# Query and key of a fused linear-attention and feed-forward block: seven block products of 256 columns in place of eight

## The reference, cut to what matters

```python
# B, N, C, H = 8, 1024, 256, 16 ; D = C // H = 16 ; INTER = 1024
xn = _layernorm(x, axis=-1)
qkv = (xn @ qkv_w + qkv_b).reshape(b, n, 3, H, D)
q, k = _l2norm(q), _l2norm(k)                  # over the 16 values of a head
kv = jnp.einsum('bhnd,bhne->bhde', k, v)
out = jnp.einsum('bhnd,bhde->bhne', q, kv)
attn = out @ proj_w + proj_b
h = jax.nn.relu(xn @ W1 + b1)
return x + attn + (h @ W2 + b2)
```

## Time and profile before

| | |
|---|---|
| median of 3 runs | 554.02 us (553.8 to 554.61) |
| profiled execution: span on the core | 552.4 us |
| around that span, against the median | 1.6 us |
| TensorE busy | 547.7 us (99%) |
| VectorE busy | 398.5 us (72%) |
| ScalarE busy | 286.9 us (52%) |
| GpSimd busy | 119.4 us (22%) |

### The profile page before, as it was taken

The page is one execution under the profiler, slowest core; times in us unless marked ns, Lnnn a source line. Parts: engine busy times, 40 slices in busy tenths (PEclk is TensorE's granted clock), DMA queues, the critical chain, the costliest instruction groups (busy, mean ns, idle before and its releaser), DMA issues.

```text
span 552.4 us, 8714 instructions
## 1 busy us (share of the span) xinstructions
PE 547.7 (99%) x2590; PEld 460.2 (83%) x2590; DVE 398.5 (72%) x791; ACT 286.9 (52%) x529; POOL 119.4 (22%) x150
## 2 busy tenths in 40 slices
PE   9999999999999999999999999999999999999997
PEld 7888888888888888888888888888888888888896
DVE  6977788567795876858667587775777767684655
ACT  4785654556336563465644556455553655533421
POOL 4242424202052020420213202331024201050100
PEclk9999999999999999999999999999999999999999
DMA  8522134343413434134341343315333251314312
GB/s 259 167 87 50 33 83 93 83 105 83 107 20 86 98 85 95 24 86 98 85 88 31 93 92 84 81 38 113 71 90 67 45 107 38 79 37 93 96 39 76
DMA packets 141413, 45.34 MB, mean 82 GB/s; under 512 B 133330, under 2 KB 136402, under 8 KB 141396
## 3 DMA queue, kind: packets, MB, share of 16 engines
q1 hardware_dynamic: 139280, 44.61, 34.7%
q10 hardware_dynamic: 2116, 0.53, 0.5%
HBM read 20.98 MB, written 8.39 MB: 53 GB/s over the span
## 4 chain that ended last, share of the span: by engine, by line
PE 99%; DVE 0%; issue 0%
PE o_bank L1169 12%; PE o_bank L1170 12%; PE o_bank L1171 12%; PE w_bank L1169 11%; PE w_bank L1170 11%; PE w_bank L1171 11%; PE v_bank L1169 7%; PE v_bank L1170 7%; PE v_bank L1171 7%; PE kv_bank L1307 3%; PE g_bank L1307 3%; PE kv_bank L1312 1%; PE g_bank L1312 1%; PE kv_bank L1323 1%; PE w_bank L1361 1%; PE g_bank L1171 0%
## 5 line engine op out<-in xcount | busy, mean ns | idle before, releaser
L957 DVE SCALAR_TENSOR_TENSOR h_lo<-w_bank,h_hi 128x512 fp32r<-128x512 f32 x128 | 87.4, 683 | 38.2 <-ACT h_hi L607 36.5
L607 ACT ACTIVATE h_hi<-w_bank 128x512 fp32r<-128x512 f32 x128 | 76.4, 597 | 66.5 <-PE w_bank L1171 66.4
L1169 PE MATMUL w_bank<-xT_hi,w_hi 128*128 128x512 f32 x254 | 99.9, 393 | 0.0
L1170 PE MATMUL w_bank<-xT_lo,w_hi 128*128 128x512 f32 x254 | 99.2, 391 | 0.0
L1171 PE MATMUL w_bank<-xT_hi,w_lo 128*128 128x512 f32 x254 | 98.9, 389 | 0.0
L1169 PE MATMUL o_bank<-h_hi,w_hi 128*128 128x512 f32 x240 | 93.5, 389 | 0.0
L1170 PE MATMUL o_bank<-h_lo,w_hi 128*128 128x512 f32 x240 | 93.4, 389 | 0.0
L1171 PE MATMUL o_bank<-h_hi,w_lo 128*128 128x512 f32 x240 | 93.4, 389 | 0.0
L405 POOL TENSOR_TENSOR xn_lo<-xn,xn_hi 128x256 fp32r<-128x256 f32 x56 | 42.5, 759 | 217.6 <-ACT xn_hi L517 213.4
L420 POOL TENSOR_TENSOR y_sb<-y_sb,y_rows 128x256 f32<-128x256 f32 x56 | 52.5, 941 | 123.7 <-DVE y_rows L1001 103.2
L585 ACT ACTIVATE qk_sq<-v_bank 128x512 f32<-128x512 f32 x64 | 38.3, 598 | 72.2 <-PE v_bank L1171 72.2
(11 more groups left out here) (213 smaller groups left out, 921.4 us busy)
## 6 DMA issues: line engine op xcount, KB each, us to landing
y_rows<-blocks SPq DMA_DIRECT2D x256, 32.0 KB, 1.9
x_sb<-x SPq DMA_DIRECT2D x15, 512.0 KB, 3.5
y_sb<-x SPq DMA_DIRECT2D x60, 128.0 KB, 3.3
out<-y_sb SPq DMA_DIRECT2D x58, 128.0 KB, 2.5
xT_raw<-blocks SPq DMA_DIRECT2D x224, 32.0 KB, 1.9
y_sb<-w SPq DMA_DIRECT2D x4, 256.0 KB, 5.1
x_sb<-x SPq DMA_DIRECT2D x2, 256.0 KB, 3.0
w_raw<-w SPq DMA_DIRECT2D x2, 256.0 KB, 7.4
```

Of the source, the lines that this page charges most:

```text
L607: nc.scalar.activation(h_hi[:, j % RING, :], w_bank[j % 2][:], ACT.Relu).then_inc(h_done, 1)
L957: nc.vector.scalar_tensor_tensor(h_lo[:, r, :], w_bank[j % 2][:], 0.0, h_hi[:, r, :].bitcast(F32), ALU.max, ALU.subtract).then_inc(h_lo_do ...
L1169: nc.tensor.matmul(to, left[0], right[0], start=first, stop=False, skip_group_check=shared)
L1170: nc.tensor.matmul(to, left[0], right[1], start=False, stop=False, skip_group_check=shared)
```

## The change

Write the 256 input channels of a tile of tokens as two blocks, and the 512 outputs (q, then k) as two blocks. The product of two tiles with all weights is then a 2 by 2 block product. Before it takes eight block products; after, from half 3 on, seven, with sums and differences of blocks of both factors and of some results (Strassen's product in Winograd's form). Tile n is paired with tile n + 2.

- TensorE: for each pair of tiles, `qk_begin`, `qk_second`, `qk_third` and `qk_fourth` issue 6, 6, 6 and 3 matmuls of 256 columns, where two `query_key` issued 12 of 512. A half has two pairs.
- GpSimd: `x_forms` makes the sums of token blocks (one instruction of 128x512 and two of 128x256, after `move_x` has landed), and `weight_forms`, once, those of the weights. They are kept in `xn` and in `wvp_raw`.
- ACT: `x_forms_high` (128x1024); `qk_seed` (two copies of 128x256, between `qk_begin` and `qk_second`).
- DVE: `x_forms_low` (128x1024); `qk_seed` and `qk_sum` (128x256 each), twice in a half, between the steps of a pair.
- All engines: the `half` of a planned order is replaced by lists written out for the second half, even, odd, last even and last odd halves.
- The call of Bacc has `dynamic_dma_scratch_size=1024`.

```diff
@@ TensorE
+            def qk_begin(s, u, n, batch):
...
+                wait(pe, qk_copied, TILES * s + 2 * n - 1)
+                product(qk_11, (xT_hi[:, u, 0, tile(n)], xT_lo[:, u, 0, tile(n)]),
+                        (wqk_hi[:, 0, 0:C], wqk_lo[:, 0, 0:C]), True, False, shared=True)
+                wait(pe, xf_lo_done, s - FORMS_FROM + 1)
+                qk_form(qk_22, X11_X01, w_form(W_FIVE), n).then_inc(qk_begun, 1)
...
+            def qk_second(s, u, n):
+                wait(pe, qk_seeded, pairs_done(s, n))
+                qk_form(qk_21, X11_X01_X00, w_form(W_SIX), n).then_inc(qk_21_sixth_in, 1)
+                product(qk_11, (xT_hi[:, u, 1, tile(n)], xT_lo[:, u, 1, tile(n)]),
+                        (wqk_hi[:, 1, 0:C], wqk_lo[:, 1, 0:C]), False, True, shared=True)
+
+            def qk_third(s, n):
+                wait(pe, qk_12_seeded, pairs_done(s, n))
+                qk_form(qk_12, X10_X11_X01_X00, (wqk_hi[:, 1, C:2 * C], wqk_lo[:, 1, C:2 * C]), n)
+                qk_form(qk_21, X01_X00, w_form(W_SEVEN), n).then_inc(qk_21_seventh_in, 1)
+
+            def qk_fourth(s, u, n):
+                wait(pe, qk_22_summed, pairs_done(s, n))
...
+            def even_half(b, s):
+                ffn_up(s, 0, 2)
+                ffn_down(s, b, 0, 0)
+                ffn_up(s, 0, 3)
+                ffn_down(s, b, 0, 1)
+                ffn_up(s, 0, 4)
+                ffn_down(s, b, 0, 2)
+                qk_begin(s + 1, 1, 0, b)
+                gather(s, b, 0)
+                qk_second(s + 1, 1, 0)
...
@@ GpSimd
+            def x_forms(s):
+
+                wait(pool, x_moved, 16 * MOVES * (s - 1))
+                first, second = slice(0, PAIR * P), slice(PAIR * P, HALF)
+                nc.gpsimd.tensor_tensor(xf_raw[:, 0:2], xT_raw[:, :, second],
+                                        xT_raw[:, 0].rearrange("p (a n) -> p a n", a=PAIRS),
+                                        ALU.subtract).then_inc(xf_sums_done, 1)
...
@@ DVE
+            def even_half(b, s):
+                divide(0, 0, q_done)
+                xT_low(s + 1, 1)
+                h_low(s, 2)
+                transpose_q(s, 0)
+                x_forms_low(s + 1)
+                k_low(s, 0)
+                h_low(s, 3)
+                variance(s + 2, b + 1, 0)
...
+            def odd_half(b, s):
...
+                sum_pair_squares(s + 1, 0, 0)
+                h_low(s, 7)
+                transpose_x(s + 2)
+                mask_kv(b)
...
```

More of the change, by code:

```diff
@@ L108, in build @@
         xT_raw = sb("xT_raw", [P, KC, HALF])
+        xf_hi, xf_lo = (sb(f"xf_{n}", [P, FORMS, PAIR * P], F32R) for n in ("hi", "lo"))
         h_hi, h_lo = (sb(f"h_{n}", [P, RING, HALF], F32R) for n in ("hi", "lo"))
@@ L164, in build @@
         second_raise = xn_first[:, 0, :]
+        qk_11, qk_22 = (v_bank[0][:, n * C:(n + 1) * C] for n in range(2))
+        qk_12, qk_21 = (v_bank[1][:, n * C:(n + 1) * C] for n in range(2))
         g_banks = [g_bank, kv_bank]
@@ L1080, in opening @@
                 divide(1, 1, k_done)
-            def half(b, s, u, last):
[L1083 to L1115, removed]
-                else:
[L1117 to L1136, removed]
-                if is_second(s):
-                    qT_low(s, u)
-                if ahead:
-                    h_low(s + 1, 1)
-                    divide(1, 1 - u, k_done)
-                else:
-                    qT_low(s, u)
@@ new lines, in second_half @@
+            def second_half():
+                ffn_up(1, 1, 2)
+                ffn_up(1, 1, 3)
+                ffn_down(1, 0, 1, 0)
+                query_key(2, 0, 0)
+                ffn_up(1, 1, 4)
+                ffn_down(1, 0, 1, 1)
+                ffn_up(1, 1, 5)
+                ffn_down(1, 0, 1, 2)
+                gather(1, 0, 1)
+                ffn_up(1, 1, 6)
+                query_key(2, 0, 1)
+                ffn_down(1, 0, 1, 3)
+                ffn_down(1, 0, 1, 4)
+                query_key(2, 0, 2)
+                key_value(0)
+                ffn_up(1, 1, 7)
+                query_key(2, 0, 3)
+                project(0)
+                ffn_up(2, 0, 0)
+                ffn_down(1, 0, 1, 5)
+                ffn_down(1, 0, 1, 6)
+                ffn_up(2, 0, 1)
+                ffn_down(1, 0, 1, 7)
@@ new lines, in odd_half @@
+            def odd_half(b, s):
+                ffn_up(s, 1, 2)
+                ffn_up(s, 1, 3)
+                ffn_down(s, b, 1, 0)
+                ffn_down(s, b, 1, 1)
+                ffn_up(s, 1, 4)
+                qk_begin(s + 1, 0, 0, b)
+                ffn_down(s, b, 1, 2)
+                qk_second(s + 1, 0, 0)
+                gather(s, b, 1)
+                ffn_up(s, 1, 5)
+                qk_third(s + 1, 0)
+                ffn_down(s, b, 1, 3)
+                qk_fourth(s + 1, 0, 0)
+                ffn_up(s, 1, 6)
+                ffn_up(s, 1, 7)
+                key_value(b)
+                qk_begin(s + 1, 0, 1, b)
+                ffn_down(s, b, 1, 4)
+                ffn_down(s, b, 1, 5)
+                ffn_up(s + 1, 0, 0)
+                qk_second(s + 1, 0, 1)
+                project(b)
+                qk_third(s + 1, 1)
+                ffn_up(s + 1, 0, 1)
+                qk_fourth(s + 1, 0, 1)
+                ffn_down(s, b, 1, 6)
+                ffn_down(s, b, 1, 7)
@@ new lines, in last_odd_half @@
+            def last_odd_half(b, s):
+                ffn_up(s, 1, 2)
+                ffn_down(s, b, 1, 0, True)
+                ffn_up(s, 1, 3)
+                ffn_down(s, b, 1, 1, True)
+                ffn_up(s, 1, 4)
+                gather(s, b, 1)
+                ffn_down(s, b, 1, 2, True)
+                ffn_up(s, 1, 5)
+                ffn_down(s, b, 1, 3, True)
+                key_value(b)
+                ffn_up(s, 1, 6)
+                ffn_up(s, 1, 7)
+                project(b)
+                ffn_down(s, b, 1, 4, True)
+                attend_first(s, b)
+                ffn_down(s, b, 1, 5, True)
+                ffn_down(s, b, 1, 6, True)
+                ffn_down(s, b, 1, 7, True)
```

496 lines of the change are left out of this document (414 added, 82 removed).

## The result

The changed kernel takes 572.25 us (median of 4 runs, 570.87 to 573.42), the kernel before 553.92 us beside it. The ratio is 1.0327, 95% interval 1.0306 to 1.0348. The forecast was 558.7 with a range to 562.5: the direction was right, the size was not. The profiled execution has a span of 569.1 us.

A forecast was written before the change was run, and what follows sets the result against it. TensorE, never waiting after its start, bounds the kernel by summed matmul distances. Span 552.4 - 3.1 (gain) + 7.0 + 0.3 + 0.3 + 0.2 (waits) = 557.1, plus 1.6 for the median, 558.7 us; range 550.7 to 562.5.

The forecast's parts named there:

- The gain: TensorE, halves 3 to 15: 42 matmuls of 256 replace 24 of 512, saving 3.1 us, bounds 1.5 and 5.7.
- borders between 256 and 512 columns: TensorE: 0.03 us added wherever a 256-column run newly borders on 512, 8 places an even half, 5 an odd one.
- `gather` of the even halves: Halves 4 to 12: VectorE's low part of k comes late beside GpSimd's row additions; TensorE waits 1.4 us each, 7.0 us.
- what it adds elsewhere, where it is hidden: New GpSimd sums, ACT copies and VectorE pair sums: costed at nothing; failed covers cost a few tenths of a us.
- the forecast's 7.8: TensorE's forecast waits: 7.0 us in even halves 4 to 12, 0.3 in half 2, 0.3 in half 14, 0.2 in the last.
- waits that name `xf_lo`: Sign against the forecast: TensorE's waits would name VectorE's low part of the token sums (or ACT's copies, or q).
- several chains are late: Rival: odd halves stall too, 1 us more in each of twelve halves, over 562.5, about 570 us; chance 0.07.
- ACT's two copies: `qk_seed`, between `qk_begin` and `qk_second`: 0.37 us each, hidden with 0.5 us of slack in the tighter, odd-half case.
- The late `move_x`: Odd halves: issued behind a later `transpose_x`, ending about 21.8 us into the half instead of 17.4, delaying GpSimd's sums.
- an upper end for five instructions of even halves: Ahead of `gather`: each two-operand VectorE instruction could wait up to 0.74 us for GpSimd; k then 2.9 us late.

The follow-up runs named there:

- no_both: The changed kernel with GpSimd's new sums (token and weight blocks) and its row additions cut to one column per instruction; 551.78 us, ratio 0.9954.
- seven_only: The kernel before with only the seven block products in halves 3 to 15, old order, no sums, no new waits; 549.89 us, ratio 0.9926.
- write_only: The changed kernel with GpSimd's token sums one column wide and the rest written by narrow memsets that read almost nothing; 564.18 us, ratio 1.019.
- half1: The changed kernel with weight sums in 256-column pieces, `project` one `ffn_up` later, q's low part ahead of the norms on VectorE; 571.18 us, ratio 1.031.
- reorder: `half1` plus, in odd halves and the last, VectorE's scaling of q moved behind the low part of k; 566.26 us, ratio 1.0236.
- all_fixes: `reorder` with even-half rows added by VectorE, GpSimd's other rows after k's low part, one `load_y` earlier, even-half q scaling later; 561.76 us, ratio 1.0149.
- before_load: The kernel before plus GpSimd's new work alone, reading weights and writing a buffer nobody reads; 558.53 us, ratio 1.007.
- no_rows: The changed kernel with only GpSimd's row additions cut to one column per instruction, its new sums whole; 558.90 us, ratio 1.0087.

## Why the forecast was right in kind and wrong in size

**The gain** was nearly right: 3.1 us forecast, 3.6 by the loop of `no_both`. Of the 5.7 us of bare distances I had taken off 2.6 for borders between 256 and 512 columns, 0.03 us each at 86 places; the 3.6 leave 2.1, 0.024 each. `seven_only` gains 4.3 because it has 52 such places; 1.4 us for them is 0.027 each.

**`gather` of the even halves** was right: 7.0 us of waits forecast for five, 6.8 measured, 7.7 with the matmuls behind them. The list of VectorE shows it, with GpSimd's 8.86 us of row additions from 229.98 on:

```profile
231.30 1.32 DVE L1145 TENSOR_TENSOR qk_even<-qk_even,qk_rn 128x1024 f32<-128x1024 f32 x1
232.55 2.38 DVE L973 TENSOR_TENSOR xT_lo<-xT_raw,xT_hi 128x512 fp32r<-128x512 f32 x2
...
236.66 1.57 DVE L973 TENSOR_TENSOR xf_lo<-xn,xf_hi 128x1024 fp32r<-128x1024 f32 x1
238.16 1.76 DVE L973 TENSOR_TENSOR k_parts<-qk_even,k_parts 128x1024 fp32r<-128x1024 f32 x1
```

Against 1.22, 1.29, 1.22 and 1.21 alone that is 2.1 us more; I had taken 2.0.

**The step that failed** is the paragraph "what it adds elsewhere, where it is hidden". There I costed GpSimd's sums at nothing because GpSimd has idle time and ends before ACT needs it. Their price isn't on GpSimd: it is on whoever on VectorE reads two SBUF operands beside them. I had used that very mechanism for the row additions, a paragraph later, and didn't ask it of the sums. In half 1 it makes 6.4 us of waits and slow matmuls, in six odd halves 6.0: together 12.4 of the 13.1 us of excess that the forecast's 7.8 lacked. The run without the sums (561.25, excess 11.4) is near the kernel that I had forecast (558.7, excess 7.8). The prediction had listed the sign: waits that name `xf_lo` would show it wrong, and six do.

**The rival "several chains are late"** (about 570, chance 0.07) gave the time and the right sign in odd halves, but for another reason: ACT's two copies were never waited for. The late `move_x` it names is probably part of the cause, since it puts the token sums beside the norms at the start of odd halves. A chance of 0.07 was too small for a list of which I had checked one place in three.

The Trainium skill, "SBUF — State Buffer", section "Who interferes with whom", says that a VectorE instruction with two inputs in SBUF and a GpSimd instruction that reads SBUF exclude each other for a whole instruction, and that one that only writes doesn't. The runs agree on both: `kv_lo` at 2.45 us instead of 0.43 beside a read of 2.39, and no lengthening beside `memset`s. I had cited it as an upper end for five instructions of even halves; the waits in half 1 and in odd halves come of the same thing.

What stays open: whether some order makes the seven products pay. With undisturbed VectorE it would be 550 to 552 us (`no_both`); the best complete order stands 9 us above. Doing the weight sums elsewhere than in half 1 wasn't tried. For the weight sums and the rows no run tells reading from being busy, as `write_only` does for the token sums.

## What to carry to other kernels

Work that is put on an idle engine is priced on the engine with which it shares a resource, so look up, instruction by instruction, what runs beside it there, and compare with that engine's slack at each due time, not with the idle time of the engine that gets the work. Moving the one who waits needn't remove the lateness of a busy in-order engine: in `half1` it was paid at the next due time, and what helped (`reorder`) was to move work that nobody needs soon behind work that is due. Measure slack by due time: in the loop the old lists absorbed the very load that cost the new lists 6 us.

## What the runs showed of the hardware that I had not expected

Tiny instructions are held up as long as large ones: `qk_e`, 128x128 and 0.28 us alone, took 1.90 us beside a GpSimd read of 2.41, and `ln_sum` of 128x4 elements 0.69 instead of 0.17 in `all_fixes`. So a long GpSimd read is worst beside small VectorE instructions. Cut into pieces of 256 columns (`half1`) the weight sums held `kv_lo` for 0.85 us instead of 2.45.

A wait of TensorE of some 2 us was in most cases followed by a stretch at the lower of its two clock levels, in some not. In the changed kernel, windows of the timeline show it (us, engines' busy time, then the granted clock PEclk):

```profile
84.00:88.00 4.00, 2.32 (x11) 1.58 (x9) 3.96 (x5) 0.00 (x0) 3.84 (x3) 1.00 1.19 209
88.50:92.30 3.80, 3.80 (x11) 3.00 (x10) 2.63 (x5) 0.72 (x1) 1.69 (x4) 0.55 0.19 27
92.30:96.00 3.70, 3.70 (x17) 3.01 (x17) 2.48 (x3) 3.23 (x5) 2.93 (x3) 1.00 0.00 0
```

From 88.5 to 92.3 the clock is 0.55, that is 1.2 GHz instead of 2.4 for nearly all of it, and matmuls of 512 columns stand 0.43 us apart instead of 0.227. That adds 1.7 us to the wait of 1.8 here, 1.6 to the 2.5 in `before_load` and 2.8 to the 4.0 in `half1`. But behind the wait of 2.4 us at 75.79 in the same execution the granted clock is 1.00 up to 88, while behind the same wait in `no_rows` it is 0.68 from 75.5 to 79.5 and the matmuls cost 1.7 us more. What decides it no run here shows.
